# Output projection widened to 84 columns, with residual and first direction accumulated in PSUM ahead of the last gating, and LayerNorm statistics read there

## What is computed

```python
x = x + deformable_conv(group_norm(x))                 # block 1
t = to_tokens(x)
u = layernorm(t)                                        # block 2 works on u; the sum below is over u
xn = layernorm(u) * gamma + beta
y  = mamba(xn, forward) + flip(mamba(flip(xn), backward)) + u
t  = t + y                                              # t + u is the residual that the kernel keeps
v  = layernorm(t)                                       # block 3
h  = v @ W_gat                                          # 16 columns: 4 heads x 4 experts
a_src = (h * att_src).sum(-1); a_dst = (h * att_dst).sum(-1)     # 4 heads each
# graph attention over 262144 edges with gathered rows [h, a_src], then layernorm, top-2 of 4 experts
out = t + sum_e gate_e * (gelu(v @ W1[e] + b1[e]) @ W2[e] + b2[e])
```

## Time and profile before

| | us |
|---|---|
| median of 3 runs (746.07 to 747.66) | 747.19 |
| the profiled execution, its own time | 746.95 |
| span of its trace | 745.2 |
| DVE busy | 610.3 (82%) |
| PE busy | 551.7 (74%) |
| ACT busy | 297.4 (40%) |
| POOL busy | 288.4 (39%) |
| mean granted PE clock | 0.821 of full speed |

### The profile page before, as it was taken

One profiled execution on the slowest core, in us unless ns is written; L12 is line 12 of the kernel. 1 busy time (PEld: TensorE's weight loads), 2 busy tenths in 40 slices (PEclk: granted clock), 3 DMA queues, 4 the chain that ended last, 5 costly groups with the idle time before them and its releaser, 6 DMA issues.

```text
span 745.2 us, 11002 instructions
## 1 busy us (share of the span) xinstructions
PE 551.7 (74%) x4083; PEld 354.4 (48%) x4083; DVE 610.3 (82%) x1196; ACT 297.4 (40%) x343; POOL 288.4 (39%) x179
## 2 busy tenths in 40 slices
PE   3578898989999986965688887798797777970040
PEld 2168787878888983421232332232233274750030
DVE  4999948576798969767899999899999727379987
ACT  2431313223123115487778555465555403320040
POOL 4033303020220200034566576566666603777304
PEclk9889796969999995987699999899999965555555
DMA  8300000000000001000000000000000000011100
GB/s 217 76 1 3 0 4 1 3 8 2 3 2 9 3 8 40 1 0 0 0 0 0 0 0 0 1 0 0 0 0 0 0 1 13 10 9 7 4 2 28
DMA packets 17585, 8.46 MB, mean 11 GB/s; under 512 B 14691, under 2 KB 16771, under 8 KB 17283
## 3 DMA queue, kind: packets, MB, share of 16 engines
q1 hardware_dynamic: 15746, 7.26, 3.7%
q0 software_dynamic: 1792, 0.58, 1.6%
HBM read 6.58 MB, written 1.25 MB: 11 GB/s over the span
## 4 chain that ended last, share of the span: by engine, by line
PE 41%; DVE 32%; issue 16%; ACT 8%; DMA 1%; DVEq 1%; POOL 0%; ACTq 0%; SPq 0%; POOLq 0%
PE ps L579 10%; PE ps L587 9%; DVE ps L1297 9%; PE ps L606 3%; PE ps L794 3%; PE ps L563 3%; DVE arena L1304 3%; PE ps L714 2%; PE ps L806 2%; PE ps L757 2%; DVE arena L1484 2%; DVE g L1486 2%; ACT arena L866 1%; PE ps L667 1%; DVE arena L1156 1%
## 5 line engine op out<-in xcount | busy, mean ns | idle before, releaser
L478 POOL TENSOR_TENSOR arena<-arena 128x1024 f32<-128x1024 f32 x64 | 150.6, 2355 | 83.9 <-DVE arena L1304 32.7
L1304 DVE TENSOR_TENSOR_SCAN arena<-arena,ps 128x1024 f32<-128x1024 f32 x64 | 146.3, 2287 | 10.3 <-ACT arena L951 2.1
L714 PE MATMUL ps<-arena,ident 128*128 128x512 f32 x256 | 128.1, 629 | 30.2 <-POOL arena L478 30.2
L450 POOL TENSOR_TENSOR arena<-arena 128x1280 f32<-128x1280 f32 x16 | 39.6, 2497 | 191.3 <-DVE arena L1171 164.7
L955 ACT ACTIVATE arena<-ps 128x1024 f32<-128x1024 f32 x64 | 65.5, 1023 | 75.6 <-POOL arena L478 55.5
L714 PEld LDWEIGHTS ps<-arena,ident 128*128 128x128 f32 x256 | 46.8, 197 | 94.2 <-POOL arena L478 54.2
L1297 DVE TENSOR_TENSOR ps<-arena,ps 128x1024 f32<-128x1024 f32 x64 | 77.3, 1208 | 2.3 <-PE ps L700 2.2
L579 PE MATMUL ps<-arena 128*128 128x64 f32 x576 | 78.8, 304 | 0.0
L951 ACT ACTIVATE arena<-arena,neg_a 128x1020 f32<-128x1020 f32 x64 | 73.2, 1144 | 9.8 <-DVE arena L1291 4.2
L579 PEld LDWEIGHTS ps<-arena 128*128 128x128 f32 x576 | 76.5, 218 | 1.2
L866 ACT ACTIVATE arena<-ps 128x768 f32<-128x768 f32 x48 | 37.3, 809 | 93.7 <-PE ps L606 93.7
(11 more groups left out here) (313 smaller groups left out, 751.0 us busy)
## 6 DMA issues: line engine op xcount, KB each, us to landing
arena<-dram_edges SPq DMA_DIRECT2D x2, 1024.0 KB, 7.5
arena<-dram_x SPq DMA_DIRECT2D x2, 512.0 KB, 5.3
arena<-node_rows,src_idx POOLq DMA_INDIRECT x56, 2.6
x_tok<-dram_x SPq DMA_DIRECT2D x1, 512.0 KB, 10.3
res_scratch<-x_tok SPq DMA_DIRECT2D x4, 128.0 KB, 2.0
arena<-res_scratch SPq DMA_DIRECT2D x1, 512.0 KB, 3.2
w<-dram_w SPq DMA_DIRECT2D x3, 128.0 KB, 2.6
out<-arena SPq DMA_DIRECT2D x1, 352.0 KB, 2.2
```

The lines of the kernel that those rows point to most:

```text
L478: g.tensor_tensor(gg[e], hh[e], cs[e], ALU.mult).then_inc(s["g_ready"], 1)
L714: m = pe.matmul(ps[:, 4 + q, :], ident[:], gg[e][:, 512 * q:512 * q + 512], start=False, stop=True, skip_group_check=True)
L1304: v.tensor_tensor_scan(o, x0, x1, 0.0, ALU.mult, ALU.add).then_inc(s["scan_ready"], 1)
```

## The change

- **20 more columns.** The projection weight `o_w[d]` grows from 64 to 84 columns (`FOLD`): 64 outputs, 16 columns that give the centred output times `W_gat`, and 4 that give its source scores. The 20 extra columns are the output weight times `fold`, a constant matrix built on the chip from `W_gat`, a centring matrix `cent` (made by POOL) and the block matrix `att_blk` of `att_src` (a new input). Five small matmuls and seven small ACT copies in the last two rounds of the convolution loop make them (`fold_psum`, `fold_ready`). SP loads `att_blk` and two transposed output weights, and `w_gat` once where it was twice.
- **Residual on PE.** After the 56-matmul sum of the payload (`pay`, L682) in stage 2, PE transposes `resb` (8 transposes into banks 4 and 5), ACT copies it to `res_t`, and `project_z(0)` waits for that copy (`rest_t_ready`).
- **Output projection in three token groups** of 6, 6 and 4 in banks 2, 3 and 0. `out_first` adds the residual (matmuls with 168 columns, two token groups at once) and the first direction (84 columns). One group is done ahead of each of the last two `add_state`, the third behind them. Only 16 matmuls of the second direction stay behind the last `gated`.
- **Statistics in PSUM.** DVE runs `bn_stats` and `bn_aggr` for each of 16 token groups straight from PSUM. `h` and `a_src` come scaled out of the same banks in three operations; `v_tok` in 16 `tensor_scalar` with mean and reciprocal deviation as pointers; `t2` is copied out behind them. The transposes L763, copies L959, matmuls L770 and the DVE operations L1337 to L1355 go.

```diff
@@ SP @@
-            sp.wait_ge(s["h_ready"], 1)
+            sp.wait_ge(s["h_ready"], 3)
             sp.dma_start(tab_d.rearrange("(p j) r -> p j r", p=P), hrow[:]).then_inc(s["tab_out"], 16)
@@ PE, convolution loop @@
+                if i == NT - 2:
+                    pe.wait_ge(s["wffn_in"], 96)
...
+                    pe.matmul(ps[0:HE, 7, 0:2 * C], w_gat[:], cent, start=True, stop=True).then_inc(s["fold_psum"], 1)
+                    pe.matmul(ps[:, 7, 192:192 + HE], cent, w_gat[:], start=True, stop=True).then_inc(s["fold_psum"], 1)
+                elif i == NT - 1:
+                    pe.wait_ge(s["fold_ready"], 5)
+                    for d in range(2):
+                        pe.matmul(ps[:, 7, 256 + 32 * d:256 + 32 * d + ROW], o_wt[d], fold[0:C, C:FOLD], start=True, stop=True).then_inc(s["fold_psum"], 1)
                 if i:
                     conv_tail(i - 1)
+                if i == NT - 2:
+                    pe.wait_ge(s["fold_ready"], 3)
+                    pe.matmul(ps[:, 7, 192 + HE:192 + ROW], wg_t, att_blk, start=True, stop=True).then_inc(s["fold_psum"], 1)
@@ PE, projections @@
             pe.wait_ge(s["hist_ready"], 1)
+            pe.wait_ge(s["res_back"], 16)
+            for a2 in range(NPO // 2):
+                m = pe.transpose(ps[:, 4 + a2 // 4, P * (a2 % 4):P * (a2 % 4) + P], resb[:, 2 * a2:2 * a2 + 2, :].rearrange("p j c -> p (j c)"), ident[:])
+            m.then_inc(s["rest_t_psum"], 1)
             project_z(0)
@@ PE, end of the scan @@
+            def out_first(grp):
+                j0, j1, bank = J_BANK[grp]
+                for j in range(j0, j1, 2):
+                    pe.matmul(ps[:, bank, FOLD * (j - j0):FOLD * (j - j0) + 2 * FOLD], res_t[:, j // 2, :], fold, start=(j == j0), stop=True,
+                              skip_group_check=True)
+                for j in range(j0, j1):
+                    pe.matmul(token_out(grp, j), zs[0][:, j:T:NPO], o_w[0][:], start=False, stop=True, skip_group_check=True)
+
+            pe.wait_ge(s["rest_t_ready"], 1)
+            pe.wait_ge(s["yg_ready"], 2)
+            pe.wait_ge(s["c_ready"], 4 * DS + 1)
+            out_first(0)
+            add_state(4 * DS - 2, 0)
+            out_first(1)
+            add_state(4 * DS - 1, 1)
+            pe.wait_ge(s["scan_ready"], 4 * DS + 1)
+            out_first(2)
             pe.wait_ge(s["yg_ready"], 4)
-            for j in range(NPO):
-                o = ps[:, 0 + j // 8, C * (j % 8):C * (j % 8) + C]
-                for d in range(2):
-                    m = pe.matmul(o, zs[d][:, j:T:NPO], o_w[d][:], start=(d == 0), stop=(d == 1))
-            m.then_inc(s["t2_psum"], 1)
+            for grp in range(3):
+                for j in range(J_BANK[grp][0], J_BANK[grp][1]):
+                    m = pe.matmul(token_out(grp, j), zs[1][:, j:T:NPO], o_w[1][:], start=False, stop=True, skip_group_check=True)
+                m.then_inc(s["t2_psum"], 1)
@@ PE, experts @@
             pe.wait_ge(s["vt_ready"], 2)
+            pe.wait_ge(s["t2_ready"], 3)
@@ ACT @@
                 if d == 0:
+                    act.wait_ge(s["rest_t_psum"], 1)
+                    f(res_t.rearrange("p a q -> p (a q)"), banks(4, 2), ACT.Copy).then_inc(s["rest_t_ready"], 1)
                     silu_z(d)
@@ DVE @@
+            for grp, (j0, j1, bank) in enumerate(J_BANK):
+                v.wait_ge(s["t2_psum"], grp + 1)
+                for j in range(j0, j1):
+                    v.bn_stats(out=st16[:, j, :], in_=tokens(grp)[:, j - j0, 0:C]).then_inc(s["stats2"], 1)
+                v.wait_ge(s["stats2"], j1)
+                for j in range(j0, j1):
+                    k.go(v.bn_aggr(out=mv16[:, j, :], in_=st16[:, j, :]))
+            k.wait()
+            ts(lns[:, 3, :], mv16[:, :, 1], 1e-5, None, ALU.add).then_inc(s["ln_var"], 1)
             v.wait_ge(s["ln_std"], 9)
             k(v.reciprocal(lns[:, 5, :], lns[:, 4, :]))
+            for grp, (j0, j1, bank) in enumerate(J_BANK):
+                tt(hrow[:, j0:j1, :], tokens(grp)[:, :, C:FOLD], bc(lns[:, 5, j0:j1], 2, ROW), ALU.mult).then_inc(s["h_ready"], 1)
+            for grp, (j0, j1, bank) in enumerate(J_BANK):
+                for j in range(j0, j1):
+                    ts(v_tok[:, j, :], tokens(grp)[:, j - j0, 0:C], mv16[:, j, 0:1], lns[:, 5, j:j + 1], ALU.subtract, ALU.mult).then_inc(s["v_ready"], 1)
+            for grp, (j0, j1, bank) in enumerate(J_BANK):
+                v.tensor_copy(t2[:, j0:j1, :], tokens(grp)[:, :, 0:C]).then_inc(s["t2_ready"], 1)
```

More of the change, by code:

```diff
@@ L128, in program @@
         diag_d = [sb(f"diag_d{d}", [P, P]) for d in range(2)]
-        o_w = [sb(f"o_w{d}", [P, C]) for d in range(2)]
+        o_w = [sb(f"o_w{d}", [P, FOLD]) for d in range(2)]
         gb = sb("gb", [P, 2])
-        w_gat = sb("w_gat", [P, 2, HE])
+        w_gat = sb("w_gat", [C, HE])
         att = sb("att", [P, 2, HE])
@@ L871, in _ @@
                     hats(i // 2)
+                if i == NT - 2:
+                    act.wait_ge(s["fold_psum"], 2)
+                    f(wg_t, ps[0:HE, 7, 0:2 * C], ACT.Copy).then_inc(s["fold_ready"], 1)
+                    for r in range(2):
+                        rr, at = slice(C * r, C * r + C), FOLD * r + C
+                        f(fold[rr, at:at + HE], ps[rr, 7, 192:192 + HE], ACT.Copy).then_inc(s["fold_ready"], 1)
                 if i >= 6 and i % 2 == 0:
                     ln_root(i // 2 - 3)
+                if i == NT - 2:
+                    act.wait_ge(s["fold_psum"], 3)
+                    for r in range(2):
+                        rr, at = slice(C * r, C * r + C), FOLD * r + C + HE
+                        f(fold[rr, at:at + HEADS], ps[rr, 7, 192 + HE:192 + ROW], ACT.Copy).then_inc(s["fold_ready"], 1)
+                elif i == NT - 1:
+                    act.wait_ge(s["fold_psum"], 5)
+                    for d in range(2):
+                        f(o_w[d][:, C:FOLD], ps[:, 7, 256 + 32 * d:256 + 32 * d + ROW], ACT.Copy).then_inc(s["fold_ready"], 1)
             ln_root(5)
@@ L1544, in laid_out @@
     }
+    r["att_blk"] = np.zeros((HE, HEADS), np.float32)
+    for h in range(HEADS):
+        r["att_blk"][EXP * h:EXP * h + EXP, h] = np.asarray(w["L1_ffn_att_src"])[h]
     for p in ("f_", "b_"):
```

100 lines of the change are left out of this document (53 added, 47 removed).

## The result

The changed kernel took 740.43 us (median of four: 734.25, 734.90, 745.97, 746.02), the kernel before on the same chip 746.63 us (median of four, 745.09 to 747.66). That is 6.2 us less at the medians, but no run lies near 740.43: two are some 12 us faster than the kernel before and two are level with it. The ratios in this document, here 0.984 with a 95% interval of 0.981 to 0.987, leave out runs that lie more than 1.5% above the fastest of their kernel (two of these four, two of six in experiment 1, three of six in 2, one of six in 5), while the medians count all runs. The profiled execution is one of the two short ones, 734.25 us with a span of 732.4 us (before 746.95 and 745.2).

A forecast was written before the change was run, and what follows sets the result against it. The prediction took the kernel's end to move with the start of the first expert round. Terms of -13.2, +2.3 and +1.2 gave -9.7 us, from 746.95 to 737.25, stated as 737.5 us for the median, range 734 to 742.5.

The forecast's parts named there:

- rival A: The terms as summed, PE's clock staying full through the last output matmuls: 735.5 to 739.5 us, chance 0.55.
- What bounds the kernel: Whole kernel: its end moves with the first expert round's start at 626.58 us; the table's gathers must not lag either.
- Loads and constants: 0: One w_gat load goes, three small ones come where SP is idle: 0; under 1 us without that cover.
- Fold matmuls, +1.2: End of the convolution: ten records at 0.12 on the path, 1.2 us later, bounds 0.5 to 2.2.
- Residual transposes, +2.3: Ahead of project_z: eight transposes, one ACT copy and two handovers, 2.3 us later, bounds 2.0 to 2.8.
- The final matmuls: Output projection: 84-column record 0.12 us, 168-column 0.17; final matmuls start at 600.2 instead of 598.02 and take 3.84 us.
- Behind them: LayerNorm to first expert round: table leaves at 607.4 instead of 622.67; first round at 613.4, 13.2 us earlier.
- The expert rounds keep their length: Expert rounds and DVE's last 85 us: length unchanged, as the clock is at 0.50 there already.
- Rival B: Clock falls during the last 16 output matmuls, which take 7.2 us: 2.5 us later, 740.0 us, chance 0.12.
- Rival C: Clock falls ahead of project_z, where PE gains a wait for ACT: 3 us, 740.5 us, chance 0.10.
- Rivals D and E: D: scalings at 0.15, fold work in slack, 734.6 us, chance 0.06. E: small DVE operations don't overlap, 740.7 us, 0.08.
- Rival F: Clock falls at 590 us, ahead of the output packets; first round at 625.3: slower, 749.3 us, chance 0.05.

The follow-up runs named there:

- experiment 1: The changed kernel run again without any edit: median 740.64 us, ratio 0.985 to the kernel before.
- 2: Changed kernel plus ten bf16 matmuls of 512 columns behind the last output matmul, in PE's wait for v_tok: 742.27 us, ratio 0.981.
- experiment 5: Changed kernel with VectorE writing the gated product in the projection's reading order, so stationary operands are contiguous, result unaltered: 738.70 us, ratio 0.983.
- experiment 4: Changed kernel with output matmuls taking 128 consecutive columns as stationary operand, tokens thereby in wrong rows: 735.29 us, ratio 0.984.
- 3: Kernel before plus eight dummy matmuls behind its last output matmul and five ahead of its second set of transposes: 747.49 us, ratio 0.998.
- 11: Changed kernel with 18 dummy matmuls of 128 columns filling PE's new wait ahead of project_z: 740.88 us, ratio 0.991.
- 12: Kernel before plus only eight transposes ahead of project_z, ACT's copy of them and PE's wait for it: 748.91 us, ratio 1.002.
- 6: Changed kernel with the residual transposes moved behind the projection to B, C and dt, their copy made by DVE: 735.39 us, ratio 0.982.
- 8: Changed kernel with gated product written in reading order, residual transposes behind the projections, and 16 dummy matmuls in four places: 732.47 us, ratio 0.979.
- 9: Changed kernel with gated product written in reading order and residual transposes behind the projections, no added matmuls: 735.19 us, ratio 0.984.
- 7: Changed kernel plus 16 dummy matmuls of 512 columns in four places where PE waits, up to the second expert round: 739.88 us, ratio 0.988.
- experiment 10: Kernel before plus 25 dummy matmuls in PE's waits between the last output matmul and the second expert round: 744.41 us, ratio 0.995.

## Why the prediction came out right, and which step was wrong

The time is within the range of 734 to 742.5, and above the bounds of rival A, the likeliest case. That the median fell there is partly luck. No run of the first four lies at 740; two lie in the range and two above it. And two errors of 5 to 6 us with opposite signs stand behind the profiled execution.

**What bounds the kernel: right, and incomplete.** Two paths run to the end. From the first expert round, at the low clock, it is 745.2 - 626.58 = 118.6 us before; 118.8 in experiment 1, 118.65 in 4 and 5, 118.7 in 3 and 11, 118.6 in 12. From the table's DMA, where DVE waits for gathers, it is 732.4 - 613.72 = 118.7 us in the changed kernel, 118.6 in 2, 118.3 in 6, 119.1 in 8, 119.0 in 9, 119.9 in 7, 120.3 in 10. The prediction said that the end moves with the first round. That holds while the rounds are at the low clock. It called the gathers "the second thing that must not lag" without a price. With 118.7 to 120.3 us behind 622.67, the table path of the kernel before ended between 741.4 and 743.0, only 2.2 to 3.8 us ahead.

**Loads and constants: 0**: nothing in the profile of the result speaks against it; no experiment tests it.

**Fold matmuls, +1.2**: inside the bounds. The last block of 272 histogram matmuls began 1.19 us earlier than before (245.43 against 246.62) and DVE's read is 0.45 later: 1.64 us. From that block to the read it is 26.7 us in the kernel before and 28.35 in the changed one, in experiment 1 too. Ten records take 1.78, or 0.18 each, between the price taken and the upper one. What the prediction did not have is the clock at 0.50 at this place, 3.3 us, in the profiles of 2, 6 and 9.

**Residual transposes, +2.3**: 2.05 at L998 (2.50 less the 0.45 of the convolution). Right, but for the drop.

**The final matmuls: this step failed.** The prediction put an 84-column record at 0.12 us, since 32 and 64 columns cost the same at the low clock and 64 cost 0.1175 at the full one. It is 0.225. Experiments 4 and 5 show the cause: the stationary operand `zs[d][:, j:T:NPO]`, read at a stride of 64 bytes, costs 0.22 us to load at either clock, and with its columns side by side the same record takes 0.12 at the full clock. The row was there. The earlier trace rows has nine records of L757 in 1.98 us at clock 1.00, 0.22 each, the very same price as the 0.221 at 0.50; the prediction read it for its clock and not for its price. And L770, whose operand is contiguous, costs the same 0.224 at 0.50: at the low clock the stride cannot be seen, and it was at the low clock that the prediction compared the two. Against their steps the packets cost 1.8 us more (14.36 us from state 61 to L820, against 10.36 + 2.2) and the last sixteen matmuls 7.19 instead of 3.84, 3.35 more. Of these 5.15 us, 1.5 came back ahead of them (state 61 is 2.0 us later than before, not 3.5) and 0.9 behind them.

**Behind them**: the tail to the table took 2.5 us instead of 3.3, since a statistic costs 0.147 us and not 0.17 and the aggregations of the first two groups hide beside PE. `v_tok` at 0.257 was right to the hundredth. The figures of the Trainium skill (VectorE: DVE Perf Modes, "The TRN2 errata") give an estimate of 0.19 us for such a statistic. Measured are 0.147 on average in a group of six, so back to back they cost less than that. From `gated`'s end (603.22) to the first round it is 16.4 us, not 13.6.

**The expert rounds keep their length: wrong, in the other direction.** Sum of the measured terms: the first round is 6.95 us earlier instead of 9.7. At the low clock's 118.65 us that gives a span of 738.3 and a time of 740.1, the middle group of experiment 1. In the profiled execution the clock rose at about 627 us and the rounds fell from 5.6 to 3.0 us. DVE's wait for the exponentials of chunk 0 shrank from 4.86 to 0.32 us (L1548 at 644.54), so that DVE's own edge work came to bind, the branch to which the prediction gave 4.86 us of room; the last gather took 1.38 us of the gain back, and 738.3 - 732.4 = 5.9 us were left. The prediction took the low clock for a given because the kernel before had it. In the profiles of 3 and 12 the kernel before kept it; experiment 10 shows that with TensorE busy in its waits it goes there too, and that without the earlier table it is worth 3.3 us.

**Rival A** had the mechanism of the first round; the middle group of times lies 0.7 to 1.6 us above its bounds. **Rival B** gave the right duration for the last sixteen matmuls, 7.2 us, for a wrong reason. The clock did fall during them, at 606.2 us, but a strided record costs the same at both clocks: in experiment 1 the sixteen take 7.18 us wholly at 1.00. **Rival C** was given 0.10 and a price of 3 us; measured are 3.3 (L699 and L707 at 10.7 instead of 7.4 us). The drop stands in the profiles of 1, 5, 7 and 12, the last of which has only this part of the change; it is absent in 6, where the wait is gone, and in 11, where it is filled. It is also absent in the changed kernel's own profile and in those of 2 and 4, which have the same wait of 1.11 us and a clock of 1.00 behind it. So the wait alone does not bring the drop every time. No profile without an unfilled wait has it at this place, but 8 has a fall that ends 1 us before `project_z`, so that the clock never drops there without the wait is likely and not shown.

**Rivals D and E** fell: the fold is not hidden, and small operations follow each other about as taken. **Rival F** did not occur: the clock is 1.00 through the packets in every profile of the changed kernel.

**Still open.** What decides in which executions the clock drops behind the wait, and rises in the expert rounds. Of the seven profiles with the unfilled wait, the four with the drop had a shorter idle time of PE ahead of the payload sum (L722; 1.83 to 1.90 us) than the three without (2.26 to 2.50); what that means was not tried. Why the end of the convolution moves by up to 8 us in the changed kernel's variants. Why experiments 7 and 11 had no run near 733. How often each group occurs; ten times of the changed kernel gave four at 733 to 735, two at 740 to 741 and four at 745 to 746. And what the fold matmuls would cost if they stood in one of PE's waits behind 276 us; that was not tried.

## What to carry to other kernels

Price a matmul by a row of the same operand layout and the same clock, not of the same width: here the stride of the stationary operand nearly doubled a record at the full clock and could not be seen at the low one, and a row at full clock in the kernel before already told. When a stage is shortened, work out the second path to the end to the same precision as the first; a gather chain 2 to 4 us behind left 3.3 us of a clock that took the rounds from 5.6 to 3.0 us. And a forecast for a kernel with a 1 us wait placed between two bursts of TensorE, or with its clock low for long, should carry both levels of the clock as cases with their prices. Three small edits (the gated product written in reading order, the transposes behind the projections, dummy matmuls in the waits) made 732.5 us out of 740.5, though by less than the sum of what each was expected to give. And a median of four that fall in two groups names no run at all: look at the single times first.

## What the runs showed of the hardware

- An fp32 record with a stationary operand of 128 x 128 read at a stride of 64 bytes takes 0.225 us at clock 1.00 (84 columns), and 0.221 at 0.50 (64 columns). Contiguous it takes 0.12 at 1.00 (84 columns, experiment 4), and 0.224 at 0.50 (32 columns, L770).
- DVE writing 1024 columns at a stride of 512 bytes, with one operand in PSUM: 1.92 us against 1.22 (experiment 5).
- The clock can fall some 2 us behind a wait of 1.11 us that stands between full bursts, and it need not: four of seven profiles with that wait, unfilled, show it. Such a drop cost 3.3 us.
- The clock can also fall while TensorE is fully busy: from 600.9 us in the kernel before, from about 270 us in the profiles of 2, 6 and 9.
- The clock came back in the expert rounds at 627 us in the changed kernel's own profile, at 628 in 6 and 625 in 9, with nothing added there; at 632 with ten bf16 matmuls in one wait (2), at 630 and 623 with 16 in four (7 and 8), at 619 with 25 in the kernel before (10). In the profiles of 1, 4, 5 and 11 it did not come back ahead of 640.
